# Probabilities times values in four 64 by 64 parts of TensorE's array, in place of two 128 by 64 parts with zero blocks

## The reference

```
q, k: [b, s, 16, 48]      v: [b, s, 16, 32]
scores = jnp.einsum('bsid,bsjd->bsij', q, k) * SCALER
attn = jax.nn.softmax(scores, axis=-1)
out = jnp.einsum('bsij,bsjd->bsid', attn, v).reshape(b, s, 512)
return out @ Wo + bo
```

## Time and profile before

| | |
|---|---|
| median of 3 runs | 2031.97 us |
| the profiled execution | 2036.26 us |
| its span, first to last instruction | 2034.3 us |
| TensorE products busy, whole span | 1891.7 us, 93% |
| VectorE busy, whole span | 1521.6 us, 75% |
| ScalarE busy, whole span | 1092.7 us, 54% |
| token pipeline in full swing, 227.3 to 1283.4 us | TensorE 1056.10 of 1056.10 us, VectorE 912.59 us |
| products of probabilities and values (L569) | 73.7 us busy, 64 tiles |
| the scaling copy (L837) | 44.2 us busy, 64 times 691 ns |

### The profile page before, as it was taken

How to read it: one execution, slowest core, us unless ns; L and a number is a source line. 1 busy time by engine, 2 the same in 40 slices (tenths; PEclk the granted TensorE clock), 3 DMA queues, 4 the chain that set the end, 5 groups by cost and what they waited for, 6 DMA issues and landing times. The chain is left out here.

```text
span 2034.3 us, 49113 instructions
## 1 busy us (share of the span) xinstructions
PE 1891.7 (93%) x14529; PEld 1501.6 (74%) x14529; DVE 1521.6 (75%) x3935; ACT 1092.7 (54%) x1745; POOL 551.3 (27%) x773
## 2 busy tenths in 40 slices
PE   5899999999999999999999999973899999978886
PEld 4788888888888888888888888863455555546564
DVE  6588888888888888888888888862444444429997
ACT  4576767666666667676666666650233223223333
POOL 1111112121111111121211111110344444427776
PEclk8799999999999999999999999997899999989998
DMA  5245454545454554545454545446699999999994
GB/s 188 68 135 141 130 151 128 149 130 152 128 147 125 143 139 133 149 128 150 130 152 128 147 125 145 128 110 194 204 294 305 295 295 302 294 338 383 404 388 178
DMA packets 414119, 384.12 MB, mean 189 GB/s; under 512 B 289712, under 2 KB 298032, under 8 KB 414000
## 3 DMA queue, kind: packets, MB, share of 16 engines
q1 hardware_dynamic: 394544, 329.83, 53.6%
q0 software_dynamic: 14336, 35.66, 7.4%
q10 hardware_dynamic: 5184, 17.96, 2.2%
HBM read 232.59 MB, written 150.77 MB: 188 GB/s over the span
## 5 line engine op out<-in xcount | busy, mean ns | idle before, releaser
L852 POOL TENSOR_SCALAR ve<-mv 128x1 f32<-128x1 f32 x192 | 43.0, 224 | 1072.1 <-DVE mv L689 1071.3
L589 ACT COPY qT<-bank 48x512 f32<-48x512 f32 x256 | 269.3, 1052 | 72.2 <-PE bank L441 67.5
L589 ACT COPY kT<-bank 48x512 f32<-48x512 f32 x256 | 269.0, 1051 | 4.7
L1060 PE MATMUL e_gu<-w,xgT 128*128 128x384 f32 x512 | 184.2, 503 | 12.8 <-DMA w<-w_ed 9.5
L448 PE MATMUL bank<-wgu,xfT 128*128 128x416 f32 x512 | 186.7, 365 | 4.5 <-ACT xfT L589 4.5
L449 PE MATMUL bank<-wgu,xfT 128*128 128x416 f32 x512 | 181.4, 354 | 0.0
L638 ACT ACTIVATE prob<-prob 128x512 f32<-128x512 f32 x128 | 78.8, 633 | 176.0 <-DVE prob L786 176.0
L465 PEld LDWEIGHTS score_ps<-kT,qT 48*64 48x64 f32 x4096 | 133.1, 138 | 40.8 <-issue 40.8
L465 PE MATMUL score_ps<-kT,qT 48*64 48x64 f32 x4096 | 150.6, 224 | 11.6 <-ACT kT L589 11.6
L1060 PEld LDWEIGHTS e_gu<-w,xgT 128*128 128x128 f32 x512 | 93.2, 192 | 71.8 <-DMA w<-w_ed 10.0
L1221 DVE SCALAR_TENSOR_TENSOR tanh<-tanh,e_gu 128x192 f32<-128x192 f32 x64 | 22.7, 355 | 165.0 <-ACT tanh L1147 165.0
(11 more groups left out here) (177 smaller groups left out, 4926.0 us busy)
## 6 DMA issues: line engine op xcount, KB each, us to landing
w<-w_eg SPq DMA_DIRECT2D x64, 768.0 KB, 6.8
acc_scratch<-zero SPq DMA_DIRECT2D x130, 256.0 KB, 4.2
w<-w_ed SPq DMA_DIRECT2D x64, 384.0 KB, 10.9
xf_scratch<-xf SPq DMA_DIRECT2D x64, 288.0 KB, 2.1
xin<-x SPq DMA_DIRECT2D x64, 256.0 KB, 3.0
v_scratch<-v SPq DMA_DIRECT2D x64, 256.0 KB, 3.8
vbd<-v_scratch SPq DMA_DIRECT2D x128, 128.0 KB, 3.2
o_scratch<-o SPq DMA_DIRECT2D x256, 64.0 KB, 2.3
```

The costliest lines, as they stand in the source:

```text
L589: nc.scalar.copy(dst, src).then_inc(done.sem, 1)
L1060: last = nc.tensor.matmul(gu_ps[par], xgT[:, par, n, :], w1[:, place, n, :], start=(n == 0), stop=(n == KD - 1))
```

## The change

Each group's product uses only its own half of the partitions: 64 partitions are contracted, the moving operand has 32 columns, and there are no zeros. Each matmul so needs a quarter of the array, and there are twice as many. Their order is n, then b, then g, and the half of the rows is h = (b + g) % 2, so that four matmuls in a row go to the four quarters in turn. Results from the upper rows go to `b4[:, 0:256]`, those from the lower rows to `s0[:, 0:256]`.

The layout of the values changes with it: block cg of the upper half and of the lower half now stand side by side in the partitions, and the load of each half writes a contiguous run of 512 floats in each partition.

VectorE's scaling copy becomes two, one for each bank, with 256 columns each, and `d_pv` counts 2 for a tile. As `s0` is now read by that copy, TensorE's transposes of xf into `s0` wait for `d_pv` of tile i-3, where they waited for ScalarE's copy of `probT`. GpSimd's memset goes, and SyncE's first load of values waits for the split of the weights that are staged in the same memory.

```
         s0, s1 = score_ps[:, 0:512], score_ps[:, 512:1024]
+        pv_ps = (b4[:, 0:256], s0[:, 0:256])
...
-        vbd = sb("vbd", [P, 2, NBLK, 2, DH])
+        v_all = sb("vbd", [P, 4 * D])
+        vbd = v_all[:, 0:2 * D].rearrange("p (a n d) -> p a n d", a=2, d=DH)
...
-        vs = vbd[:].rearrange("p a n b d -> p (a n b d)")
+        vs = v_all[:]
...
-        d_pv = count("d_pv")
+        d_pv = count("d_pv", 2)
...
                 if isinstance(i, int) and i == 1:
-                    sp.wait_ge(zeroed, 3)
+                    sp.wait_ge(part_lo, KD + 3 + KD)
...
                     for b in range(2):
-                        sp.dma_start(vbd[64 * b:64 * b + 64, 1 - par, :, b, :], src[b]).then_inc(v_in[1 - par].sem, 16)
+                        sp.dma_start(vbd[64 * b:64 * b + 64, 1 - par], src[b]).then_inc(v_in[1 - par].sem, 16)
...
                 if active(i - 5):
                     pe.wait_ge(d_ln[2].sem, d_ln[2].at(i - 5))
-                    pe.wait_ge(a_pT.sem, a_pT.at(i - 3, 1))
+                    pe.wait_ge(d_pv.sem, d_pv.at(i - 3))
                     transposes(s0, [xf[:, 1 - par, n * P:(n + 1) * P] for n in range(KD)], pe_xfT)
...
                     pe.wait_ge(a_pT.sem, a_pT.at(i - 3))
+                    pe.wait_ge(d_pv.sem, d_pv.at(i - 3))
                     settle(pe)
                     scores(range(0, NBLK // 2)).then_inc(pe_s.sem, 1)
...
                     for n in range(8):
-                        for g in range(2):
-                            last = nc.tensor.matmul(b4[64 * g:64 * g + 64, n * 64:n * 64 + 64],
-                                                    probT[:, n, 64 * g:64 * g + 64],
-                                                    vbd[:, par, 2 * n + g].rearrange("p b d -> p (b d)"),
-                                                    start=True, stop=True)
+                        for b in range(2):
+                            for g in range(2):
+                                h = (b + g) % 2
+                                last = nc.tensor.matmul(pv_ps[h][64 * g:64 * g + 64, n * DH:n * DH + DH],
+                                                        probT[64 * h:64 * h + 64, n, 64 * g:64 * g + 64],
+                                                        vbd[64 * h:64 * h + 64, par, 2 * n + g],
+                                                        start=True, stop=True)
...
-                    nc.vector.tensor_tensor(o[:].rearrange("p (n d) -> p n d", d=DH),
-                                            b4[:].rearrange("p (n d) -> p n d", d=DH),
-                                            srec[:].unsqueeze(2).broadcast_to([P, NBLK, DH]), ALU.mult).then_inc(d_pv.sem, 1)
+                    for b in range(2):
+                        nc.vector.tensor_tensor(o[:].rearrange("p (n b d) -> p b n d", b=2, d=DH)[:, b],
+                                                pv_ps[b].rearrange("p (n d) -> p n d", d=DH),
+                                                srec[:].rearrange("p (n b) -> p b n", b=2)[:, b].unsqueeze(2).broadcast_to(
+                                                    [P, NBLK // 2, DH]), ALU.mult).then_inc(d_pv.sem, 1)
...
-                if isinstance(i, int) and i == 0:
-                    pool.wait_ge(part_lo, 11)
-                    nc.gpsimd.memset(vbd[:], 0.0).then_inc(zeroed, 1)
```

## The result

The kernel after takes 2060.13 us in the median of four runs (2047.03 to 2065.46), the kernel before, beside it on the same chip, 2032.6 us (2031.49 to 2041.35). The ratio is 1.0111, with a 95% interval of 1.0081 to 1.014: slower by 1.1%. The profiled execution took 2059.84 us, 23.6 more than that of before. 2051 us had been predicted, with a range of 2036 to 2064.

A forecast was written before the change was run, and what follows sets the result against it. TensorE was taken to set the pace, VectorE near behind. A net stall of 0.31 us for 57 tiles (17.7) plus 1.4 once gave 19 us on 2031.97, so 2051 us; own range 2042 to 2062, with rivals 2036 to 2064.

The forecast's parts named there:

- Step 1: VectorE's scaling copy ends after TensorE's transposes of xf now start, by a mean of 0.21 us.
- Step 2: Splitting VectorE's 512-column scaling copy into two of 256 takes 0.76 us instead of 0.69, adding 0.07.
- Step 3: Release from VectorE's end of the copy to TensorE's load for xf's transposes takes 0.05 us.
- Step 4: After the wait, the first load of xf's transposes can't run ahead of its product: 0.06 us exposed.
- Step 5: TensorE's bubble of 0.08 us before the `wgu` product is filled by the delay, giving 0.08 back.
- Step 6: VectorE's chain shifts with TensorE and reaches the scaling copy no earlier: 0 us back, bound 0.1.
- The burst, no gain because the load decides: Product of probabilities and values: 64 loads in four parallel parts take the time of 32 in two, no gain.
- Rival one: Only two array parts run at once: burst grows 1.04 us, 1.0 us a tile, about 2092 us; chance 0.11.
- Rival three: Product gets faster and TensorE keeps the gain: half the burst, 0.46 us a tile, 2006 us; chance 0.07.
- TensorE's own path then gets 0.06 us longer ... it turns out to cost nothing: Array-part switch before the product of probabilities and values adds 0.06 us a tile, hidden by the wait at xf's transposes.
- 0.31 for a turn: Net stall at TensorE's transposes of xf per tile: 0.39 less 0.08 us, bounds 0.17 to 0.50.
- The tail, 1.4 us once: At the pipeline's end, the last transposes wait for the split copy, delaying TensorE's low products by 1.4 us once.

The follow-up runs named there:

- experiment 1: Kernel after with the banks of the rank product and lower-row results exchanged, so xf's transposes wait for ScalarE's copies as before: 2049.7 us, ratio 1.0064.
- experiment 2: Kernel before with only the changed wait, xf's transposes waiting for the one scaling copy of tile i-3, old product kept: 2049.93 us, ratio 1.0082.
- experiment 6: experiment 1 with each product loading 32 instead of 64 columns of probT, leaving out half the result's rows: 2022.89 us in one run.
- experiment 7: experiment 1 with the same 64 products ordered quarter after quarter instead of in turn: 2242.48 us in one run.
- experiment 4: Kernel after, unchanged, run once more in the same job as other variants: 2058.63 us, ratio 1.013 against the kernel before.
- experiment 8: Kernel after with the first half of k's transposes (0.44 us) moved ahead of those of xf: 2045.9 us, ratio 1.0024 against the kernel before.
- experiment 9: Kernel before with token-pipeline iterations written out to 57, only 58 to 61 left in the hardware loop: 2031.17 us, ratio 0.9974.

## Why the prediction was right, and where it was off

It forecast slower by 19 us, and it is slower by 24 to 28 (profile and median). The mechanism was the one named, the wait for the scaling copies, but it was only about half of the cost: 0.13 of 0.28 us for a turn by the distances, 0.125 by experiment 1.

- **Step 1, the copy ends 0.21 after the transposes' start: right.** It is 0.18 and 0.24 in turn over the 50 turns of the trace before.
- **Step 2, the copy in two: right.** From 711.07 to 711.82 are 0.75 us, 0.76 said.
- **Step 3, 0.05 for the release: too small.** In each turn with the full wait, in experiment 2 as in the kernel after, the load starts 0.115 us after the copy's end.
- **Step 4, no load ahead: right.** After the full wait the load starts only 0.03 ahead of its product and the transposes of xf take 0.03 longer, 0.06 in all, as said.
- **Step 5, the bubble before `wgu`: right, but half of what comes back.** From `wv` to `wgu` it is 0.077 shorter in both kinds of turns, 0.08 said. Behind the full wait another 0.075 goes between the first and the second `wgu` product (0.263 us before, 0.186 in experiment 2), which nothing in the prediction names. This and step 3 are misses of nearly one size and cancel; that experiment 2 gives 0.235 where the steps give 0.24 is luck to that extent.
- **Step 6, nothing comes back from VectorE: right for the wait alone** (experiment 2). In the change itself it went otherwise, for a reason that isn't VectorE: in every second turn TensorE comes 0.2 us later by itself.
- **The burst, no gain because the load decides: right**, by experiment 6 (0.56 us for half the columns) and by the burst's own 0.92 us. Rival one, only two parts at once, falls with experiment 7, where one quarter at a time takes more than three times as long. Rival three, a faster product, falls with the same window of L574.
- **"TensorE's own path then gets 0.06 us longer ... it turns out to cost nothing": this is the step that failed.** The path got 0.15 longer (experiment 1: 0.153). The switch was sized right for this loop, 0.05; the loop's end wasn't seen, 0.21 in every second turn. And that it costs nothing held only in part: with the wait in place, the product adds 20.986 - 20.943 = 0.043 to the turn, which is less than the 0.07 of the split copy. So the number of 0.31 for a turn came out near 0.278 because the wait hides TensorE's lateness as said; but the sentence that the product isn't in the loop is wrong for every second turn. That the loop's end costs about what the wait would have cost in that turn is luck, and it is why the sum of two causes comes out so near to the one that was priced. Whoever had removed the wait on its word would have found half of the loss still there.
- **The tail, 1.4 us once: not there.** The last transposes do wait, and as long as foreseen (1363.47 to 1367.06 are 3.6 us, 3.65 measured):

```profile
1382.89 1.09 PE L443 MATMUL score_ps<-c,xf 128*128 128x128 f32 x4 [3.65 <-DVE o L843]
...
1396.50 0.24 PE L564 MATMUL score_ps<-tri,chosen 128*64 128x128 bf16 x1 [0.92 <-DVE chosen L809]
1396.67 0.66 PE L443 MATMUL score_ps<-c,xf 128*128 128x128 f32 x4
```

  But the transposes of the next tile start at 1396.67, against 1381.10 before:

```profile
1380.92 0.24 PE L561 MATMUL score_ps<-tri,chosen 128*64 128x128 bf16 x1 [0.92 <-DVE chosen L804]
1381.10 0.66 PE L441 MATMUL score_ps<-c,xf 128*128 128x128 f32 x4
```

  That is 15.6 later, what the turns had cost, so nothing of the wait gets through. TensorE has slack at the end of the pipeline, where VectorE's `chosen` releases it in both kernels.
- **The total.** 57 x 0.278 = 15.8, less 0.4 at the end, is 15.4 to the first product of the experts, where 19 were said. The rest of the profile's 23.6 is 8.2 us behind the token pipeline. Experiment 4 shows the experts' stage vary by 12 us between two executions of one kernel; yet its median, 24.7 us above before, is more than the pipeline's 15.4 too. 1.3 us lie behind the experts (experiment 4). Why the medians keep some 8 to 11 more that no changed instruction explains isn't settled: experiments 1 and 8 have the same period, and the one is 15.8 us above before in its job and the other 5.6. So the 2060 us owe as much to what the forecast doesn't name.
- **Two slips in the working, without effect here.** The lower ends of the steps give 0.18 + 0.05 + 0.05 + 0.03 - 0.08 - 0.1 = 0.13, not 0.17. And the first rival is counted with 60 turns, the forecast with 57.

## What to carry to other kernels

Before a small matmul is cut into more and smaller ones, ask whether the load or the moving columns set its pace: a quarter of the array does each load no faster, so four quarters at once only buy back the doubled number of instructions. Count the records too: at the end of a hardware loop the instructions queued ahead seem to be what covers the jump (argued below), and twice as many short ones left 0.21 us of it uncovered here. And where a result moves to another bank, look up who writes that bank next and how late its reader is; here a swap of two banks, or 0.44 us of other work put ahead of the wait, takes away all of the wait's cost.

## What the runs showed of the hardware

- **The jump at the end of a loop.** First product of the burst to the first of q: 1.291 us where the 128 instructions of the burst take 0.92, 1.09 where they take 0.56, and no more than in any other turn, 1.08, with 64 instructions of 0.93. The difference between the first two, 0.20, is near half of that between the bursts, 0.36. So it looks as if the sequencer could issue the last instruction of the burst only when about half of them had run, and from there the jump took some 0.8 us: 0.46 + 0.83 and 0.28 + 0.81. With 64 instructions all would be issued before the burst begins. Experiment 7 fits: half of its burst of 3.08 us is 1.54, more than 0.8, and its loop's end costs nothing. This is argued from these numbers and wasn't tried by itself. The Trainium skill (TensorE: Matmul & The Clock Gate, section Architectural detail: the array is 16× 32×32, not 1× 128×128) gives TensorE a queue of 64, and half of 128 fits that.
- **Loads and products of quarters.** In each quarter a load of 64 columns starts every 0.058 us with four quarters in turn, and every 0.049 us with one quarter alone. Four at once bring 3.14 / 0.92 = 3.4 times.
- **A switch of the array's parts** costs 0.14 us from load to load (0.17 against 0.03).
- **The clock** fell to 0.56 in the 2.1 us behind a burst that used one quarter at a time for 3.2 us; with all four in turn it stayed at 1.00. In experiment 9 it read 0.50 from 566.1 to 569.0, after TensorE had waited 0.69 us for a transfer, up to 564.26, and worked again for 1.8 us. The length of such a wait alone doesn't decide it: one of 1.12 us, up to 917.9, wasn't followed by a lower clock.
- **Written-out iterations** of the kernel before are 0.154 us shorter in the median (20.554 against 20.709) and lose it all again in 7 of 47 turns, by a late reload of `o` in each and a lower clock in two. The two places that got shorter are the bubble before `wgu` (0.08) and the one between the rank product and the burst (0.07).
